# Fourth attention: the second maxima of a turn placed ahead of the input statistics on VectorE

## What is computed

```
x = x + tanh(g_xattn[i]) * xattn_i(layernorm(x), ctx)
x = x + tanh(g_ffn[i])   * ffn_i(layernorm(x))
```

```
q, k, v = Q @ w_q.T + b_q, K @ w_k.T + b_k, V @ w_v.T + b_v
attn = softmax(q k^T / sqrt(16)); out = (attn v) @ w_o.T + b_o
```

## Time and profile before

| | |
|---|---|
| median of 3 executions | 2732.43 us (2729.92 to 2735.24) |
| profiled execution | 2728.43 us, span 2726.6 us |
| PE busy | 2442.1 us (90%) |
| DVE busy | 1358.7 us (50%) |
| ACT busy | 944.1 us (35%) |
| POOL busy | 576.3 us (21%) |
| mean granted clock of TensorE | 0.945 |

### The profile page before, as it was taken

The page is one execution under the profiler, slowest core; times in us unless marked ns, Lnnn a source line. Parts: engine busy times, 40 slices in busy tenths (PEclk is TensorE's granted clock), DMA queues, the critical chain, the costliest instruction groups (busy, mean ns, idle before and its releaser), DMA issues. The chain is left out here.

```text
span 2726.6 us, 39284 instructions
## 1 busy us (share of the span) xinstructions
PE 2442.1 (90%) x13940; PEld 1603.5 (59%) x13940; DVE 1358.7 (50%) x3016; ACT 944.1 (35%) x2203; POOL 576.3 (21%) x544
## 2 busy tenths in 40 slices
PE   7997999999899987987999889967985799999998
PEld 4444776666666654444666655434554577777776
DVE  6985655754545546864232743254875323232232
ACT  2465555444444432322222212224543222222221
POOL 3233222440001002103221100002354211121121
PEclk9998999999999998998999579988997899999999
DMA  5012001220001002000000059002013422222121
GB/s 185 7 34 97 17 9 47 71 78 24 24 24 45 26 13 76 1 1 16 0 0 33 0 191 331 31 4 97 32 63 147 135 36 32 32 35 34 32 34 26
DMA packets 73747, 144.42 MB, mean 53 GB/s; under 512 B 11592, under 2 KB 62536, under 8 KB 71120
## 3 DMA queue, kind: packets, MB, share of 16 engines
q1 hardware_dynamic: 41280, 100.94, 10.8%
q0 software_dynamic: 16368, 26.23, 4.9%
q10 hardware_dynamic: 15936, 15.03, 1.9%
HBM read 107.42 MB, written 71.09 MB: 65 GB/s over the span
## 5 line engine op out<-in xcount | busy, mean ns | idle before, releaser
L1937 PE MATMUL PS<-mem,ctx2T 128*128 x1136 | 350.0, 461 | 2.0 <-ACT ctx2T L2000 1.2
L1937 PEld LDWEIGHTS PS<-mem,ctx2T 128*128 128x128 f32 x1136 | 211.4, 191 | 108.8 <-issue 4.3
L318 POOL TENSOR_TENSOR rstd<-var_eps,minus_half 128x4 f32<-128x4 f32 x50 | 51.9, 1039 | 784.0 <-DVE var_eps L275 505.6
L2119 POOL DMA_INDIRECT out_x<-xnT,moe_small x71 | 110.2, 1553 | 486.0 <-ACT xnT L2014 486.0
L1959 PE MATMUL PS<-mem,moe_small 128*128 x852 | 195.7, 379 | 1.1 <-DVE moe_small L2091 1.1
L2083 DVE TENSOR_TENSOR ctx2T<-PS,ctx2T 128x352 f32<-128x352 f32 x142 | 74.5, 525 | 244.7 <-PE PS L1937 244.7
L1040 DVE RECIPROCAL mem<-PS 128x512 f32<-128x512 f32 x48 | 160.8, 3351 | 14.7 <-PE PS L629 13.4
L1959 PEld LDWEIGHTS PS<-mem,moe_small 128*128 128x128 f32 x852 | 156.4, 190 | 19.9 <-issue 1.4
L2713 DVE TENSOR_REDUCE moe_small<-PS 128x2 f32<-128x1024 f32 x64 | 78.5, 1226 | 141.5 <-PE PS L2385 141.5
L1035 DVE TENSOR_REDUCE mem<-PS 128x32 f32<-128x2048 f32 x48 | 109.9, 2290 | 73.7 <-PE PS L585 67.9
L2552 ACT ACTIVATE mem<-PS,moe_small 128x512 f32<-128x512 f32 x128 | 86.8, 683 | 156.8 <-DVE moe_small L2713 133.2
(11 more groups left out here) (361 smaller groups left out, 4699.0 us busy)
## 6 DMA issues: line engine op xcount, KB each, us to landing
slots<-in_trash_rows SPq DMA_DIRECT2D x8, 4290.0 KB, 62.8
mem<-in_L_ffn_experts SPq DMA_DIRECT2D x8, 2176.0 KB, 8.9
xn<-unit_rows SPq DMA_DIRECT2D x15, 512.0 KB, 3.8
xn<-slots ACTq DMA_DIRECT2D x53, 130.0 KB, 2.1
x_all<-in_x SPq DMA_DIRECT2D x8, 512.0 KB, 8.4
mem<-unit_rows SPq DMA_DIRECT2D x8, 512.0 KB
out_x<-x_all ACTq DMA_DIRECT2D x8, 512.0 KB
unit_rows<-moe_small SPq DMA_DIRECT2D x7, 512.0 KB, 2.9
```

What stands on the lines that cost most here:

```text
L1937: last = nc.tensor.matmul(PS[:, 1 + 2 * g + half, 0:HE], m.rowT[:, j % 2, k, :], w[:, :, at:at + HE], start=k == 0, stop=k == KD - 1)
L2119: nc.gpsimd.indirect_dma_start(s.T["out"], bass.IndirectOffsetOnAxis(s.token[:, j % 4:j % 4 + 1], 0), m.result[:, j % 4, :], None, compute ...
```

## The change

In the fourth attention, in turns 0 to 5, DVE runs `maxima(n, 1)` ahead of `stats(n + 2)` where before it ran them the other way round. The other three attentions keep their order, and no other engine's program is touched.

```diff
@@ -1164,10 +1164,12 @@
             normalise(n - 2, 1)
         if route:
             norm_scales(n - 3)
-        if n + 2 < B:
+        if n + 2 < B and not m:
             stats(n + 2)
         if now:
             maxima(n, 1)
+        if n + 2 < B and m:
+            stats(n + 2)
         if n == 0:
             place_values(2)
             place_values(3)
```

## The result

The changed kernel took 2743.19 us (median of 5, 2742.69 to 2745.09) against 2732.43 before (median of 5, 2729.92 to 2735.24): ratio 1.0046 [1.0034, 1.0057], **slower by 10.8 us**. The profiled execution took 2743.14 (span 2741.3). Lines behind L1172 stand 2 higher in the changed kernel (add_bias L1211, scatter L1242).

The account below looks back on a forecast made before the run. PE and DVE waiting for each other in turn in the fourth attention were taken as the bound. Terms 1.5 + 2.0 + 2.0 - 0.2 + 0 - 0.7 + 1.2 = +5.8 on 2732.43 gave 2738.2 us; own range 2736 to 2740, wide 2729.5 to 2746.5.

Parts of the forecast that it names:

- rival (a): Turns 4 and 5: POOL's later scatters meet PE's results, 1.5 to 4 us per turn, 2741 to 2746; chance 0.17.
- Turns 0, 1 and 2, +1.5, +2.0, +2.0: Statistics behind the second maxima delay DVE work that PE's L597 waits for: +1.5, +2.0 and +2.0 us.
- Clock, +1.2: PE's new waits in turns 0 to 2 bring between one half and one fall to half clock, 1.6 us each: +1.2.
- Turn 3, -0.2: Maxima start 1.2 us earlier, PE's 0.84 wait at L605 goes, DVE then idles 0.8 for scores: -0.2 us.
- Turn 4, 0: Maxima start no earlier; the reciprocal's 2.0 us delay is swallowed by DVE's 2.84 idle before L1092: 0.
- turn 5, -0.7: POOL's add_bias moves later, so L1097 is no longer stretched and ends near 1992.7, not 1993.4: -0.7 us.
- (c): Turns 4 to 6: shifted waits avoid turn 4's clock fall, paying back 3 to 5 us, 2733 to 2735; chance 0.15.
- Rival (b): Turn 5's later add_bias holds a two-input operation of place_rows, delaying turn 6's first maxima: +2.3, 2740.5; chance 0.08.
- Rival (d): Turns 4 and 5: maxima start when scores are issued, within 1.5 us of L585's in turn 4; 2727 to 2729; chance 0.08.
- Rival (e): The order on DVE makes no difference, since it waits elsewhere in each turn: 2732.4; chance 0.02.

Follow-up runs that it names:

- filler: Changed kernel plus fourteen unused identity transposes on PE ahead of L597's wait, turns 0 to 2: 2723.51 us against 2710.07; with add_bias ahead of xn_scales too: 2732.03 against 2731.84.
- the second group: Runs on a faster chip: the kernel before, unedited, profiled at 2710.42 us; the changed kernel, unedited, 2723.99 against 2710.26, ratio 1.0053.
- taking add_bias away: Changed kernel with POOL's add_bias(n + 1) moved ahead of xn_scales(n + 2) from turn 3 on: 2717.42 us against 2710.26, ratio 1.0026.
- the last run: Kernel before with stats(n + 2) behind normalise(n - 1, 0) in turns 3 to 5 and add_bias ahead of xn_scales from turn 3: 2731.21 us, ratio 0.9999.
- statistics behind normalise, first group: Kernel before with stats(n + 2) moved behind normalise(n - 1, 0) in turns 3 to 5, add_bias not moved: 2713.96 us against 2710.07, ratio 1.0012.

## Why the prediction was right, and where it was off

The prediction said 2738.2, slower by 5.8; it was 2743.2, slower by 10.8. The sign held, and so did the mechanism in turns 0 to 3. The measurement lies within the wide range (2729.5 to 2746.5) but 3.2 us above the forecast's own (2736 to 2740). That it falls where rival (a) was priced (2741 to 2746) is chance: that mechanism wasn't seen. By its own steps:

- **Turns 0, 1 and 2, +1.5, +2.0, +2.0: right, shown.** With the clock held the three turns came out 5.7 us longer, against 5.5 by the sum. The waits at L597 are the forecast ones to 0.2 us, in every run with the swapped order there and no filler.
- **Clock, +1.2: the term that was mis-sized.** I priced one half to one fall out of three possible. All three came, in the profile after and in each of the four other profiled runs with this order and no filler: TensorE is at 0.50 behind every new wait, and it costs 4.4 us. What misled me was the row of turn 5, a wait of 2.80 us with no fall behind it. The nearer row, turn 4 with 2.22 us and a fall, was the better guide here. A fall isn't certain behind a wait of this length, though: behind 2.20 in turn 4 of the profile after, and behind the 2.94 of the changed kernel in the second group, the clock stayed at 1.00 for the next 4 us. Taking all three falls at the row's 1.6 would have given 4.8.
- **Turn 3, -0.2:** measured 22.6 against 23.1. L605's wait went and DVE idles 0.71 for the scores, as forecast (0.8).
- **Turn 4, 0, and turn 5, -0.7:** the maxima came 3.9 us after the scores' issue, as said, and L1097 was free, as said. But the two turns together with turn 6 are 4.2 us longer in the profiles. The long stretch at half clock moved from turn 4 to turn 5 (10 us at 0.50 from 1995.3 on) and so was not won back: (c) didn't come. And add_bias, gone from L1097 in turn 5, held L1084 for 1.82 us in turn 4, where I had looked for nothing; the kernel before had lost part of this at L1097 already (0.67 us, from 1963.60). How much of this is the order and how much the execution stays open: the two medians are 4 us closer than the two profiles. By the medians the whole loss is about what turns 0 to 2 lost (10.8 and 10.1), so on this chip the whole time doesn't test what the sum put down for turns 4 and 5.
- **Rival (b)** had the right mechanism and too small a scope. I looked for it in turn 5 only, and there, on the first chip, it missed: add_bias ended at 2006.96, and L1065 began at 2008.18. On the faster chips it comes in both turns (in the filler's run as L1084 in turn 4); taking add_bias away was worth 6.6 us to the changed kernel.
- **Rival (d)**, the faster case: on the first chip its condition wasn't met (3.92 us from L585's issue, not 1.5). On the faster chip it was, and turn 4 of the changed kernel took 25.1 us and not 23.7; with add_bias away it is neither gain nor loss (23.2 and 23.1). **Rival (e)** fell with turns 0 to 2. **Rival (a)**, scatters meeting PE's results, had no run of its own, but its sign is missing in the profile after: scatters 4 to 8 of turn 4 start 18.5 us behind the first maxima, not 14.2, and still L851 and `add_out` follow PE at once, as said there.

By the medians the halves don't add up: +12.1 and +5.6 are 17.7, and the change on a chip of that kind cost 13.7. In the profiles they do, up to turn 7. From the first maxima of turn 0 to those of turn 7 the kernel before takes 147.7 us (profile of the second group), the half of turns 0 to 2 takes 157.8 (+10.1), the half of turns 3 to 5 takes 150.7 (+3.0) and the whole change 160.7 (+13.0). The profiled executions as a whole are 10.2, 4.6 and 13.6 above that of the kernel before. So the 4 us don't lie in turns 0 to 6; most of them look like the scatter of executions, which isn't shown.

## What to carry to other kernels

Where two engines wait for each other in turn, look for each piece of work at which of them waits around it: the statistics stood in a wait of DVE for PE (3.46 and 4.80 us) and cost nothing, and behind the maxima the same 2 us stood ahead of what PE waits for. Price each new wait of TensorE with a possible fall of its clock: here 5.8 us of new waiting cost 4.4 more in five profiles out of five, though other waits as long had no fall behind them. When an order shifts by some microseconds, lay the long POOL instruction beside every short DVE instruction near it, in every turn; moving that one POOL instruction within its turn gave the only kernel of this study whose interval lies wholly below the kernel before.

## What the runs showed of the hardware that I had not expected

- The same program differs by 22 us between chips by the medians, 12 of it in turns 4 to 6, in which scatters run (83.6 and 71.3 us). On the first kind the profile calls the maxima's releases remote and they come after up to 3.1 us of idle (4.2 in one turn of the last run), on the other the kernel before starts the maxima at once behind the statistics, or 0.4 us later for L585 in turn 6. Why is open; no run here takes the scatters away.
- L1084, which adds a constant to four elements per partition and has one tensor as its input (0.16 us by itself), took 0.82 us in turn 4 on one chip and 1.82 on the other. It ended at 1962.92 and 1978.92, and add_bias ended at 1962.88 and 1978.89. L1124, again with one input, was held for 1.55 and 1.58 us (statistics behind normalise, first group). So an operation with a single input is held too; I had looked only at those with two. The Trainium skill ("SBUF — State Buffer", "Who interferes with whom") lists this kind of operation among those that can take the pair of ports shared with GpSimd; which mode it ran in no row shows.
- The indirect DMAs that POOL issues beside the same small DVE operations didn't stretch them: with add_bias away from it L1065 took 0.16 (0.19 once) in turns 4 and 5, in the time of the scatters.
